# The rotated query as three passes over weights that stand twice in the columns, instead of two passes over high and low weights side by side

## What is computed

```
q_big = (layernorm(x) @ Wq[h].T) @ w_kc_q[h]          # 512 x 384 per batch
q_big = q_big * cos + rotate_half(q_big) * sin
q_r   = q_big @ W_qr[h]                               # 512 x 64   <- the group C below
k_r   = rotary(ctx) @ W_kr[h]                         # 1024 x 64
attn  = softmax(q_r @ k_r.T)
out  += ((attn @ rotary(ctx)) @ w_kc_kv[h].T) @ Wo[h].T
```

## Time and profile before

| | |
|---|---|
| time, median of 3 runs | 848.12 us (846.5 to 849.08) |
| the profiled execution's own time | 844.1 us |
| span in the profile | 842.3 us, mean granted TensorE clock 0.974 |
| TensorE busy (matmul) | 751.9 us, 3268 matmuls |
| VectorE busy | 761.8 us, 1026 instructions |
| ScalarE busy | 573.9 us |
| GpSimd busy | 578.4 us |
| DMA | 118.54 MB, mean 141 GB/s |

### The profile page before, as it was taken

How to read it: one execution, slowest core, us unless ns; L and a number is a source line. 1 busy time by engine, 2 the same in 40 slices (tenths; PEclk the granted TensorE clock), 3 DMA queues, 4 the chain that set the end, 5 groups by cost and what they waited for, 6 DMA issues and landing times.

```text
span 842.3 us, 13224 instructions
## 1 busy us (share of the span) xinstructions
PE 751.9 (89%) x3268; PEld 480.8 (57%) x3268; DVE 761.8 (90%) x1026; ACT 573.9 (68%) x838; POOL 578.4 (69%) x581
## 2 busy tenths in 40 slices
PE   3678999999999999999999999999999686868996
PEld 2545666766666666666666666666666442424453
DVE  5899999999999999999999999999999767887896
ACT  2587677767776877687677777776777577774332
POOL 4769684968496758776776768586849475967462
PEclk9999999999999999999999999999999797979999
DMA  9226887785768486859676767677669999400001
GB/s 327 81 72 112 166 150 135 144 173 125 155 130 177 104 173 131 173 115 175 124 151 141 153 132 152 140 153 148 139 147 217 240 230 261 182 0 26 13 25 38
DMA packets 298503, 118.54 MB, mean 141 GB/s; under 512 B 275952, under 2 KB 282096, under 8 KB 298224
## 3 DMA queue, kind: packets, MB, share of 16 engines
q1 hardware_dynamic: 297664, 116.70, 63.9%
q10 hardware_dynamic: 816, 1.57, 0.5%
HBM read 49.02 MB, written 2.10 MB: 61 GB/s over the span
## 4 chain that ended last, share of the span: by engine, by line
DVE 39%; PE 32%; issue 16%; ACT 7%; POOL 3%; DMA 1%; DVEq 1%; SPq 0%; ACTq 0%; POOLq 0%
PE banks L1519 9%; DVE neg_max L1328 9%; DVE rows L1339 6%; PE scores L1760 5%; PE banks L1460 3%; PE scores L1547 3%; DVE acc L1323 3%; PE banks L1775 3%; DVE cv_lo L1293 2%; DVE rot_sin L1302 2%; DVE rest L1275 2%; DVE rot_cos L1300 2%; ACT rows L1201 2%; PE banks L1474 1%; PE banks L1492 1%
## 5 line engine op out<-in xcount | busy, mean ns | idle before, releaser
L1190 ACT ACTIVATE scores<-scores,neg_max 128x1024 f32<-128x1024 f32 x128 | 139.1, 1087 | 61.6 <-DVE neg_max L1328 61.1
L1519 PE MATMUL banks<-pt,v_hi 128*128 128x512 f16 x512 | 162.0, 383 | 11.8 <-DMA pt<-rows 7.5
L1339 DVE SCALAR_TENSOR_TENSOR rows<-scores,rows 128x1024 f16<-128x1024 f32 x128 | 154.6, 1218 | 16.4 <-ACT rows L1201 15.2
L1328 DVE TENSOR_REDUCE neg_max<-scores 128x1 f32<-128x1024 f32 x128 | 155.2, 1213 | 2.9 <-PE scores L1547 2.7
L1060 POOL TENSOR_TENSOR rot_cos<-rot_cos,rot_sin 128x512 f32<-128x512 f32 x93 | 119.1, 1281 | 42.6 <-DVE rot_sin L1302 37.7
L1201 ACT ACTIVATE rows<-scores 128x1024 f16<-128x1024 f32 x128 | 131.0, 1023 | 5.2
L1068 POOL TENSOR_TENSOR rot_lo<-rot_cos,rot_hi 128x512 fp32r<-128x512 f32 x93 | 119.9, 1290 | 7.7
L1519 PE MATMUL banks<-pt,v_lo 128*128 128x512 f16 x256 | 98.7, 386 | 0.0
L1323 DVE SCALAR_TENSOR_TENSOR acc<-banks,inv,acc 128x512 f32<-128x512 f32 x128 | 91.2, 743 | 6.1 <-PE banks L1529 2.2
L1519 PEld LDWEIGHTS banks<-pt,v_hi 128*128 128x128 f16 x512 | 49.3, 98 | 80.6 <-issue 31.7
L1164 ACT CAST cv_hi<-banks 128x512 fp32r<-128x512 f32 x64 | 37.5, 587 | 83.6 <-PE banks L1460 42.0
(11 more groups left out here) (213 smaller groups left out, 1788.5 us busy)
## 6 DMA issues: line engine op xcount, KB each, us to landing
load<-in_pack SPq DMA_DIRECT2D x15, 320.0 KB, 3.0
raw_chunk<-in_out_w SPq DMA_DIRECT2D x8, 512.0 KB, 5.1
raw_chunk<-in_gate_w SPq DMA_DIRECT2D x8, 512.0 KB, 4.6
raw_chunk<-in_val_w SPq DMA_DIRECT2D x8, 512.0 KB, 4.0
pt<-rows SPq DMA_TRANSPOSE x256, 3.3
raw<-in_gate_w SPq DMA_DIRECT2D x8, 512.0 KB, 5.4
raw<-in_val_w SPq DMA_DIRECT2D x8, 512.0 KB, 5.0
raw<-in_out_w SPq DMA_DIRECT2D x8, 512.0 KB, 7.2
```

The costliest lines, as they stand in the source:

```text
L1190: nc.scalar.activation(scores[:, u % 2, :], scores[:, u % 2, :], ACT.Exp, bias=neg_max[:, u:u + 1], accum_out=sums[:, u:u + 1]).then_inc(e ...
L1328: nc.vector.tensor_reduce(neg_max[:, u:u + 1], scores[:, u % 2, :], AX, ALU.max, negate=True).then_inc(max_ready, 1)
L1339: nc.vector.scalar_tensor_tensor(out=rows[:, u % ROWS, 1, :], in0=scores[:, u % 2, :], scalar=WEIGHT_LIFT, in1=rows[:, u % ROWS, 0, :], op ...
L1519: mm = nc.tensor.matmul(out, t[x][:, b * LC + c, :], pt[:, b, :, low * LC + c, :], start=n == 0, stop=n == 3 * LC - 1)
```

## The change

Group C is made from weights that stand twice in the columns. wr holds for each chunk a tile of high weights and a tile of low weights, each with its 64 columns twice. Three passes a chunk (high x rot_hi, low x rot_hi, high x rot_lo) give the whole value in all 128 rows of the bank. ScalarE makes one copy of 128 rows into qr_hi, VectorE one subtraction into qr_lo. The buffer rest, the "double" items and their two semaphores go; a score tile waits for VectorE's C group instead. GpSimd makes two copies and two subtractions of wr for one each. wr takes 1536 bytes more of each partition, so the identity in bf16 lies over space that is free after the heads, and is written at the start of the feed-forward's first tile. The lists are unchanged but for the "double" items.

```
@@ weight_splits @@
     def rotated(h, src):
-        split(h, 2, [t["wr"][:, :, half, :] for half in range(2)],
-              src[:, 0:CQ * R].rearrange("p (c r) -> p c r", c=CQ)).then_inc(wr_ready, 1)
+        wr, plain = t["wr"], src[:, 0:CQ * R].rearrange("p (c r) -> p c r", c=CQ)
+        for twin in range(2):
+            ins = nc.gpsimd.tensor_scalar(wr[:, :, 0, twin, :], plain, 1.0, 0.0, ALU.mult, ALU.add)
+        ins.then_inc(t["split_hi"], 1)
+        pool.wait_ge(t["split_hi"], h.after(5, 3))
+        for twin in range(2):
+            ins = nc.gpsimd.tensor_tensor(wr[:, :, 1, twin, :], plain, wr[:, :, 0, twin, :].bitcast(F32), ALU.subtract)
+        ins.then_inc(wr_ready, 1)
@@ high_part (ScalarE) @@
                 elif kind == "C":
-                    src = banks[0:R, p.bank[marked], :]
-                    nc.scalar.copy(qr[0][0:R, group[1], :], src)
-                    out = qr[0][R:2 * R, group[1], :]
+                    out = qr[0][:, group[1], :]
@@ scalar_heads @@
-            def double(p, marked):
-                b = marked[1]
-                done = p.earlier(("C", b, "next")) if marked[-1] == "last" else p.place(("C", *marked[1:]))
-                act.wait_ge(group_read, p.read(done))
-                nc.scalar.copy(qr[1][0:R, b, :], qr[1][R:2 * R, b, :]).then_inc(doubled, 1)
@@ take_out (VectorE) @@
                     if kind == "C":
-                        b, low = group[1], slice(R, 2 * R)
-                        nc.vector.tensor_tensor(rest[low, b, :], banks[0:R, bank, :], qr[0][0:R, b, :].bitcast(F32),
-                                                ALU.subtract).then_inc(rest_ready, 1)
-                        dve.wait_ge(rest_ready, h.after(B, b + 1))
-                        return nc.vector.tensor_tensor(qr[1][low, b, :], banks[low, bank, :], rest[low, b, :], ALU.add)
-                    if kind == "K":
+                        pair = [x[:, group[1], :] for x in qr]
+                    elif kind == "K":
@@ products (TensorE) @@
-                        for half in range(2):
-                            if half:
-                                pe.wait_ge(rot_ready, h.after(2 * CQ, CQ * group[1] + c + 1))
-                            mm = nc.tensor.matmul(out, wr[:, c].rearrange("p o r -> p (o r)"), rot[half][:, c, :],
-                                                  start=c + half == 0, stop=c + half == CQ)
+                        hi, lo = (wr[:, c, half].rearrange("p o r -> p (o r)") for half in range(2))
+                        nc.tensor.matmul(out, hi, rot[0][:, c, :], start=c == 0, stop=False)
+                        nc.tensor.matmul(out, lo, rot[0][:, c, :], start=False, stop=False)
+                        pe.wait_ge(rot_ready, h.after(2 * CQ, CQ * group[1] + c + 1))
+                        mm = nc.tensor.matmul(out, hi, rot[1][:, c, :], start=False, stop=c == CQ - 1)
@@ score_tile (TensorE) @@
+                places = [p.place(("C", b)) if p.first else p.earlier(("C", b, "next"))]
                 if not odd:
                     here = b or p.first
-                    pe.wait_ge(group_read, p.read(*(p.place(("K", b, half)) if here else p.earlier(("K", 0, half, "next"))
-                                                    for half in range(2))))
-                pe.wait_ge(doubled, p.head.after(B, b + 1))
+                    places += [p.place(("K", b, half)) if here else p.earlier(("K", 0, half, "next")) for half in range(2)]
+                pe.wait_ge(group_read, p.read(*places))
@@ buffers @@
-            t["wr"] = early.enter_context(nc.sbuf_tensor("wr", [P, CQ, 2, R], F32R, side="right"))
+            t["wr"] = early.enter_context(nc.sbuf_tensor("wr", [P, CQ, 2, 2, R], F32R, side="right"))
```

More of the change, by code:

```diff
@@ L74 @@
 A0, A1, V1, V0, C0, C1 = ("A", 0, "next"), ("A", 1, "next"), ("V", 1, "last"), ("V", 0), ("C", 0, "next"), ("C", 1, "next")
-UNGROUPED = ("score", "max", "exp", "sum", "double", "abs", "drop", "stats", "spread", "root", "deviation", "norm", "extreme", "scale", "X", "take", "first root",
+UNGROUPED = ("score", "max", "exp", "sum", "abs", "drop", "stats", "spread", "root", "deviation", "norm", "extreme", "scale", "X", "take", "first root",
              "turn", "start root", "values", "count", "variance", "inverse", "normed", "rotate", "products", "rotated",
@@ L102 @@
     ("high", 7, "last"), ("K", 1, 0), A0, ("K", 1, 1), ("exp", 0), ("high", 0), ("exp", 1), ("high", 1),
-    ("B", 0, 2, "next"), V1, ("exp", 2), ("high", 2), ("exp", 3), ("double", 1, "last"), ("high", 3), A1, ("abs", 2),
-    ("M",), ("exp", 4), ("high", 4), C0, ("exp", 5), ("high", 5), ("B", 1, 2, "next"), ("double", 0, "next"), V0,
+    ("B", 0, 2, "next"), V1, ("exp", 2), ("high", 2), ("exp", 3), ("high", 3), A1, ("abs", 2),
+    ("M",), ("exp", 4), ("high", 4), C0, ("exp", 5), ("high", 5), ("B", 1, 2, "next"), V0,
     ("exp", 6), ("high", 6), ("exp", 7), C1,
@@ L108 @@
     ("high", 7, "last"), A0, ("exp", 0), ("high", 0), ("exp", 1), ("high", 1), ("B", 0, 2, "next"), V1, ("exp", 2),
-    ("high", 2), ("exp", 3), ("high", 3), ("double", 1, "last"), A1, ("M",), ("abs", 0), ("exp", 4), C0, ("high", 4),
-    ("exp", 5), ("high", 5), ("K", 0, 0, "next"), ("K", 0, 1, "next"), ("B", 1, 2, "next"), V0, ("double", 0, "next"),
+    ("high", 2), ("exp", 3), ("high", 3), A1, ("M",), ("abs", 0), ("exp", 4), C0, ("high", 4),
+    ("exp", 5), ("high", 5), ("K", 0, 0, "next"), ("K", 0, 1, "next"), ("B", 1, 2, "next"), V0,
     ("exp", 6), ("high", 6), ("abs", 1), ("exp", 7), C1,
@@ L143 @@
     ("turn", "x", 4), ("turn", "x", 5), ("turn", "k", 1), ("abs", 2), ("rotate", 0, 0), ("rotate", 0, 1),
-    ("rotate", 0, 2), ("A", 1), ("abs", 0), ("C", 0), ("turn", "k", 0), ("double", 0), ("abs", 1), ("spread most",),
-    A0, ("K", 0, 0), ("K", 0, 1), ("Y", 3), ("values", 0), ("values", 1), ("C", 1), ("exp", 0), ("double", 1),
+    ("rotate", 0, 2), ("A", 1), ("abs", 0), ("C", 0), ("turn", "k", 0), ("abs", 1), ("spread most",),
+    A0, ("K", 0, 0), ("K", 0, 1), ("Y", 3), ("values", 0), ("values", 1), ("C", 1), ("exp", 0),
     ("high", 0), ("exp", 1), ("high", 1), ("Y", 2), ("K", 1, 1), ("M",), ("B", 0, 2, "next"), ("exp", 2), ("high", 2),
     ("K", 1, 0), ("exp", 3), ("high", 3), A1, ("exp", 4), ("high", 4), C0, ("exp", 5), ("high", 5),
-    ("B", 1, 2, "next"), ("double", 0, "next"), V0, ("exp", 6), ("high", 6), ("exp", 7), C1,
+    ("B", 1, 2, "next"), V0, ("exp", 6), ("high", 6), ("exp", 7), C1,
 )
@@ L171 @@
     ("high", 7, "last"), ("exp", 0), ("high", 0), ("exp", 1), ("high", 1), ("exp", 2), ("drop", 0), ("high", 2), V1,
-    ("double", 1, "last"), ("exp", 3), ("high", 3), ("exp", 4), ("high", 4), ("drop", 1), ("exp", 5), ("high", 5),
+    ("exp", 3), ("high", 3), ("exp", 4), ("high", 4), ("drop", 1), ("exp", 5), ("high", 5),
     ("drop", 2), ("exp", 6), ("drop", 3), ("M",), ("high", 6), V0, ("exp", 7), ("first root",), ("high", 7),
@@ L1976, in tile @@
                 pool.wait_ge(out_bias_loaded, 16)
+                nc.gpsimd.tensor_copy(t["ident_b"][:], t["ident"][:])
             if h.i is not None:
```

13 lines of the change are left out of this document (4 added, 9 removed).

## The result

| | before | after |
|---|---|---|
| time, median | 847.01 us (14 runs, 843.9 to 849.75) | 850.37 us (14 runs, 849.28 to 851.99) |
| ratio after to before | | 1.0042, 95% interval 1.0029 to 1.0055 |
| the profiled execution's own time | 844.1 us | 850.32 us |
| span in its profile | 842.3 us | 848.5 us, mean granted TensorE clock 0.976 |

The change costs 3.4 us, 0.4%. The forecast was 848.5 with a range of 843 to 857, and "no net effect" (within 2.5 us) as the likeliest case. The time lies in the range. The difference of 3.4 us lies outside "no net effect", on the side of rival B: slightly slower, a little over the 0.3% that a measurement can tell.

The account below looks back on a forecast made before the run. Neither VectorE nor TensorE is full; they take turns. Opening -1.5 and seven iterations +1.4 give about 0: profiled 844.1 becomes 844.0, 848.0 at the median, set to 848.5 for likely upward error; range 843 to 857.

Parts of the forecast that it names:

- no net effect: Whole kernel: time stays within 2.5 us, 846 to 851; the forecast itself, chance 0.45.
- rival B: Loop's end: filled stalls come back behind, delaying A0 and cv_lo; iteration +1.3 us, kernel 856 us; chance 0.35.
- The opening: Before the loop, VectorE is the chain with two C groups: -1.5 us, ends -2.5 and 0.
- VectorE's relief turns into idle time: Next loop junction: VectorE could be 1.0 us early but waits for A0; idle time from 4 to 7 or 8 us.
- Rival A: Loop: VectorE is the bound and its relief comes through, -1.8 us per iteration, 834 us; chance with its half-way case 0.2.
- half-way case: Loop: forced stalls shrink too, -0.7 us per iteration, 842 us; chance 0.2 together with Rival A.
- Floor of TensorE: Loop: matmuls at 0.230 (f32) and 0.216 us (f16) fill 75.5 of 81.5 us; the change adds 2.76 us.
- The iteration: One loop iteration: 2.76 us of added matmuls against 2.7 us of removable stalls, +0.2 us, ends -0.2 and +2.2.
- Step (3): Odd head: C0's subtraction ends 0.45 us earlier, K's 0.80 stall is filled by 0.69, K copies come unchanged.
- Step (4): Next junction: cv_lo of A0 has 0.2 us of slack; TensorE arrives 0.0 to 0.3 later (1.38 added, 1.15 filled).
- The loop's end: Around C1's last rot_lo pass: stalls of 0.59 us before it and 0.47 behind, where the loop branches, counted as removable.
- (1): From 309.6 us TensorE is the chain with C0 in it: +0.69 us at V0's end.

Follow-up runs that it names:

- e6: Changed kernel with A0's last part ahead of K(1,1) in TensorE's list of the even head: 845.71 us, ratio 0.9978 to before.
- e9: Changed kernel with C0's second part behind B(1,0) and its third behind score 5 in TensorE's odd-head list: 849.19 us, ratio 1.001 to before.
- e11: e9 with ScalarE's copy of C0 also moved behind high 4 in the odd head: 847.03 us, ratio 0.9999 to before.
- e8: Kernel before the change with A0's last part ahead of K(1,1) in TensorE's even-head list, as in e6: 849.14 us, ratio 0.9998 to before.
- e3: Changed kernel with GpSimd's split of wr made by one copy and one subtraction, reading the 64 columns twice: 849.93 us, ratio 1.0033 to before.
- e1: Changed kernel without the third pass (low weights x rot_hi) in group C, single copy and subtraction kept: 841.38 us, ratio 0.9925 to before.
- e5: Changed kernel with C0 of the odd heads back in the old two-pass form, with its old copies, subtractions and double: 845.86 us, ratio 0.9978 to before.
- e12: Changed kernel with the changes of e5, e6 and e11 together: 837.19 us, ratio 0.9889 to before.

## Why the prediction was nearly right, and where it failed

**The opening**, -1.5 forecast: -1.2 between the two traces. The sign is borne out, the size only roughly: head 1 begins at 91.36, 91.47, 92.54 and 91.39 in after, e6, e9 and e11, which share the changed opening, and at 92.52 and 94.63 in before and e8, which share the old one.

**GpSimd at nothing**: right, by e3. **ScalarE's relief worth nothing beyond "high 7"**: no run takes it apart from VectorE's. ScalarE is idle for (494.40 - 328.83)/6 = 27.6 us of an iteration after.

**VectorE's relief turns into idle time**: right. It stands still for 3.5 us more per iteration (3.8 to 7.3): its records are (465.97 - 450.45)/6 = 2.6 us less, and the iteration is 0.94 longer. The idle time stands where the forecast put it, before cv_lo and before the low parts. The costliest groups (busy us, mean ns, idle time before them), before:

```profile
L1339 DVE SCALAR_TENSOR_TENSOR rows<-scores,rows 128x1024 f16<-128x1024 f32 x128 | 154.6, 1218 | 16.4 <-ACT rows L1201 15.2
L1293 DVE TENSOR_TENSOR cv_lo<-banks,cv_hi 128x512 fp32r<-128x512 f32 x64 | 43.8, 684 | 15.4 <-ACT cv_hi L1164 15.1
```

and after:

```profile
L1325 DVE SCALAR_TENSOR_TENSOR rows<-scores,rows 128x1024 f16<-128x1024 f32 x128 | 156.0, 1219 | 24.0 <-ACT rows L1195 23.4
L1279 DVE TENSOR_TENSOR cv_lo<-banks,cv_hi 128x512 fp32r<-128x512 f32 x64 | 44.0, 687 | 31.2 <-ACT cv_hi L1165 31.2
```

The idle time ahead of cv_lo doubled, from 15.4 to 31.2 us. Rival A, by which the relief comes through, falls: its price was -1.8 per iteration (its own terms, 0.69 - 2.4, give -1.7), and e1 shows -0.69 even without any added pass. Its half-way case, -0.7 with the passes, falls too: with them it is +0.94.

**The step of each relief, 0.96 us per group**: the subtraction now steps 363.45 to 364.04 = 0.59, and the maximum ahead of it 362.31 to 363.45 = 1.14, where it was 1.24 with 0.72 and 0.73 behind the earlier trace rows. That is the forecast's 1.56 less 0.60. By the rule that the prediction cites from the Trainium skill (page "VectorE: DVE Perf Modes", section "Two Vector instructions with no wait between them"), the neighbour's 0.11 had to come back once the subtraction starts in the same quadrant, a group of 32 partitions, as the maximum ahead of it. The trace agrees, 0.10.

**Floor of TensorE**: right. 346 matmuls at the forecast's steps are 78.3 us, and the stalls read one by one come to 3.8 of the 4.1 that this leaves. At the loop's end of the changed kernel 333.21 to 335.03 is eight steps, 0.2275 us each. The Trainium skill (page "TensorE: Matmul & The Clock Gate", section "Back-to-back issue gap") gives a sustained 131 ns for a matmul of 512 columns. The rows again do not show it.

**The iteration, +0.2 forecast, +0.94 measured**: here it failed. I counted 2.7 us of stalls that can vanish against 2.76 of work, and took nearly all of them as filled; 1.8 were, net of a new one. The prediction's own signs say the same: the iteration was to be 81.5 to 82.0 us and is 82.40, and the stalls stayed at 4.1 where over 4 was to mean rival B. The parts:
- Step (3), "The K copies come at the same time as before". They came 0.46 later, measured from the M group. I had seen that max 5 would start 0.4 later (it was 0.65) and that C0's subtraction ends earlier, but I followed only VectorE's own order. Behind max 5 stand exp 5 and high 5 on ScalarE, and VectorE's low 5 waits for them. The K subtractions, cv_lo and with it O(0,0) queue behind low 5. A stall of 0.80 was filled and one of 0.55 appeared 7 us later. e11 shows it: with the cause gone the iteration is 0.55 shorter.
- Step (4), TensorE arriving at A0 "0.0 to 0.3 later": the copy of A0 started 0.78 later against the M group, for which 1.15 of filled stalls had been set against 1.38 of work. 1.38 - 1.15 + 0.55 = 0.78: this is the new stall before O(0,0) again, and no further cause. In e11, without that stall, the copy is 0.24 later (379.55 less 356.12, against 23.19 before), which is 1.38 - 1.15.
- The loop's end: I counted the 0.47 behind C1 among the stalls that can vanish. 0.39 of it remained although the passes ahead of it run without a wait now; the stall of 0.59 ahead of it had only made it 0.08 longer. With the 0.55 of the new stall, less 0.2 by which the forced stalls shrank, this makes up the missing 0.74.
- C0 in the even head's list: its 0.69 lies on the path with no stall near it (e5, 0.63), in keeping with (1).

**Rival B** named the right family (filled stalls come back behind) and the wrong place. It put the return at the loop's end; 0.78 of lateness does arrive at A0, but the stall that returned stands before O(0,0) of the odd head. Its +1.3 is above the measured +0.94.

**The level**: in the traces after is 6.2 us above before, where the steps gave -0.1; the medians differ by 3.4 only. I had added 4.0 us to carry the trace to the medians, and the profiled execution of after stands at its own median, where nothing is to be added. So 848.5 is only 1.9 below 850.37 by luck, because two errors offset each other: the loop's 0.74 x 7 = 5.2 that was missing, and the 4.0 that was too much.

The record says something of what sets one execution some 3 us apart from another, and in the traces it isn't the loop. Before and e8 share the opening, and their iterations are 81.46 and 81.47 us at a granted clock of 1.00. Head 1 begins 2.11 us later in e8, which is nearly all of the 2.2 us between the two profiled executions. In e8 TensorE stood still for 2.08 us up to 42.88, and from 44 us on its granted clock was at the lower level, 1.2 GHz, for some 3 us (0.51 in the stretch from 44 to 46, 0.64 in the next two us), with steps of 0.42 us for 0.23. In before it had stood still from 40 to 42 us too, and the clock stayed at 1.00. The profiled execution of e6, 3.2 us above its median, loses its time behind the heads (184.4 us from head 15's first maximum, 181.4 in after).

The runs agree with this. Over the 17 executions of before timed beside e11 and e12 the time goes with the mean granted clock: 843.5 us at 0.98, 849.44 at 0.962, correlation -0.91. The median of this clock was 0.966 to 0.968 for before on the three chips of the experiments, and 0.972 for after, e3, e6, e9 and e11, which have all the added passes. By the slopes of before's own executions (3.2 to 4.7 us for 0.01 of clock) that is worth an estimated 1.4 to 2.8 us, much of the gap between +6.2 in the traces and +3.4 in the medians. So the medians alone make the change look cheaper than it is in the loop. That the added passes raised the clock wasn't tested.

In the experiments' forecasts my errors have a common sense: the relief alone was overrated (-1.0 expected, -0.69 measured), and so was the price of the passes alone (+1.8 expected, +1.46 measured). In both I had taken each stall as either wholly filled or wholly kept; that this is the cause of the errors isn't shown.

## What to carry to other kernels

Where two engines are each busy over 90% of a loop and take turns, relief on one and work on the other are not exchanged one for one: here, per iteration, 3.8 us off VectorE were worth 0.7, and 2.76 us onto TensorE cost 1.5, and which part counts depends on each place in the order. Count a stall as filled only after following the late item through every engine that it passes (here score, max, exp, high, low) to the next wait of the engine that did the work. A relief pays once the lists are moved to fit it, the reader's list along with the writer's: the same exchange was worth 0.64 us with the relief and nothing without it, and moving TensorE's list alone gave 0.09 where moving ScalarE's with it gave 0.55.

## What the runs showed of the hardware

- At the loop's end TensorE loses about 0.3 us even where its passes run dense up to it (335.03 to 335.55 for a step of 0.23), with 0.10 more on the next step; e6 and e11 show the same (0.30 and 0.28 over the step, 0.10 on the next). The profile names no release there, and only register instructions and the branch stand between; that the branch is the cause wasn't tested by itself.
- A TensorE step right behind a stall is 0.10 to 0.11 longer in most places read (382.98 to 383.32 is 0.34 for 0.23; in the kernel before 380.15 to 380.48 is 0.33), so that a short wait costs more than its own length.
- On GpSimd a copy of twice the columns took 513 ns for 352, and a subtraction 999 for 591: 1.46 and 1.69 times, with the source read twice. From the two widths, an estimate: some 0.19 us for the instruction itself, and 0.84 and 2.1 ns for each column.
- 17 executions of before on one chip took 843.5 to 849.44 us, and a longer one mostly shows a lower mean granted TensorE clock (correlation -0.91), while the loop's six iterations ran at 1.00 in every trace kept.
- The same opening had TensorE at 1.00 from 42 to 48 us in one execution (before) and partly at the 1.2 GHz level in another (e8), behind a stall of about 2 us in both.
